# Seven products for eight: up and gate of a feed-forward layer by Strassen's blocks, with a row swap through DRAM

## What is computed

```python
x = fwht(x * SU_ug) / SCALE                        # 2048 rows x 512, "rotated"
x_up = x @ W_up.T * (Wscale_ug[:INTER] * SCALE)    # INTER = 2048
x_gate = x @ W_gate.T * (Wscale_ug[INTER:] * SCALE)
x = jax.nn.silu(x_gate) * x_up
x = fwht(x * SU_dp) / SCALE
x = x @ W_down.T * (Wscale_dp * SCALE)             # back to width 512, added to the rows
```

## Time and profile before

| | us |
|---|---|
| median of 3 runs (1525.26 to 1638.5) | 1525.43 |
| the profiled execution | 1520.79 |
| its span, first to last instruction | 1519.0 |
| granted TensorE clock, mean | 0.992 of full |

### The profile page before, as it was taken

How to read it: one execution, slowest core, us unless ns; L and a number is a source line. 1 busy time by engine, 2 the same in 40 slices (tenths; PEclk the granted TensorE clock), 3 DMA queues, 4 the chain that set the end, 5 groups by cost and what they waited for, 6 DMA issues and landing times. The chain is left out here.

```text
span 1519.0 us, 25272 instructions
## 1 busy us (share of the span) xinstructions
PE 1459.3 (96%) x10520; PEld 988.2 (65%) x10520; DVE 997.7 (66%) x1552; ACT 748.3 (49%) x926; POOL 46.1 (3%) x66
## 2 busy tenths in 40 slices
PE   6999999899999999999899999999999999999998
PEld 5886333677333687333687333677888888888886
DVE  5853999786999784999784999573333324334333
ACT  4344899335999435899335999322221212112111
POOL 1000000110000100000100000100000000000000
PEclk9999999999999999999999999999999999999999
DMA  8453000555000443000543300631010101000002
GB/s 267 151 186 125 9 10 9 153 170 194 9 9 10 153 142 139 9 10 9 154 150 148 157 10 9 200 120 56 28 55 2 56 0 55 28 28 28 1 28 83
DMA packets 53051, 120.01 MB, mean 79 GB/s; under 512 B 11472, under 2 KB 33248, under 8 KB 48080
## 3 DMA queue, kind: packets, MB, share of 16 engines
q1 hardware_dynamic: 41632, 69.94, 13.4%
q0 software_dynamic: 11312, 48.55, 10.1%
HBM read 81.56 MB, written 36.90 MB: 78 GB/s over the span
## 5 line engine op out<-in xcount | busy, mean ns | idle before, releaser
L958 ACT ACTIVATE cx_probs<-cx_sc,proj_mbias 128x1024 f32<-128x1024 f32 (+1 forms) x416 | 442.3, 1113 | 43.8 <-PE cx_sc L1221 34.8
L1103 DVE TENSOR_SCALAR cx_probs<-cx_probs 128x1024 f32<-128x1024 f32 (+1 forms) x416 | 269.9, 685 | 55.4 <-ACT cx_probs L958 54.0
L1065 DVE TENSOR_TENSOR cx_padd<-cx_probs,cx_probs 128x1024 f32<-128x1024 f32 x192 | 233.9, 1218 | 1.2 <-DVE cx_probs L1103 0.4
L1221 PEld LDWEIGHTS cx_sc<-cx_q,cx_kt 32*128 32x128 f32 (+1 forms) x2496 | 102.9, 182 | 197.1 <-ACT cx_probs L958 180.3
L1234 PE MATMUL cx_acc<-cx_probs,cx_vt 128*32 128x512 f32 (+1 forms) x1664 | 220.4, 602 | 3.8 <-DVE cx_probs L1103 3.8
L1221 PE MATMUL cx_sc<-cx_q,cx_kt 32*128 32x512 f32 (+1 forms) x2496 | 204.8, 430 | 14.7 <-ACT cx_probs L958 11.3
L136 PE MATMUL cx_sc<-proj_cs,proj_wk 128*128 128x256 f32 (+1 forms) x1152 | 148.7, 289 | 11.2 <-DVE proj_wk L614 11.2
L136 PEld LDWEIGHTS cx_sc<-proj_cs,proj_wk 128*128 128x128 f32 x1152 | 146.2, 192 | 14.2 <-issue 12.9
L136 PE MATMUL cx_sc<-proj_wv,proj_cs 128*128 128x512 f32 (+1 forms) x624 | 150.4, 397 | 5.2 <-DVE cx_kt L1048 5.2
L136 PEld LDWEIGHTS cx_sc<-proj_wv,proj_cs 128*128 128x128 f32 (+1 forms) x624 | 113.5, 184 | 35.3 <-DVE cx_kt L1048 5.4
L1246 PE MATMUL cx_tot<-cx_padd,cx_ones 128*32 128x256 f32 x1536 | 120.9, 390 | 0.0
(11 more groups left out here) (238 smaller groups left out, 1678.3 us busy)
## 6 DMA issues: line engine op xcount, KB each, us to landing
proj_raw<-in_ctxT SPq DMA_DIRECT2D x20, 512.0 KB, 4.8
scr_q<-cx_q SPq DMA_DIRECT2D x3, 2048.0 KB, 7.1
cx_wo<-scr_wo POOLq DMA_DIRECT2D x3, 2048.0 KB, 14.0
scr_xs<-cx_xs POOLq DMA_DIRECT2D x3, 2048.0 KB, 7.9
cx_q<-scr_q SPq DMA_DIRECT2D x3, 1536.0 KB, 9.1
cx_qxt<-in_x SPq DMA_DIRECT2D x4, 1024.0 KB, 8.9
scr_wd<-cx_wdhi POOLq DMA_DIRECT2D x4, 1024.0 KB, 6.6
scr_wd<-cx_wdlo POOLq DMA_DIRECT2D x4, 1024.0 KB, 8.2
```

The lines of the kernel that those rows point to most:

```text
L958: nc.scalar.activation(prob(N)[0:r], sc[n % NSC][0:r], ACT.Exp, bias=mbias[0:r, b, t:t + 1], scale=SCALE).then_inc(exp_done, 1)
L1065: nc.vector.tensor_tensor(padd[z][(g * QP + j) % 2][:], prob(2 * i + z)[:], prob(2 * i + 2 + z)[:], ALU.add).then_inc(added[z], 1)
L1103: nc.vector.tensor_scalar(prob(N)[0:r], prob(N)[0:r], LOW, HIGH, ALU.max, ALU.min).then_inc(clip_done, 1)
L1221: last = nc.tensor.matmul(sc[(2 * i + h // 2) % NSC][0:r, h % 2], kt[own, z, c, t * P:t * P + r], q[own, y, c], start=n == 0, stop=n == 2)
```

## The change

All groups but the first (groups 1 to 7) compute up and gate in another way. The stage is now a pair of batches in a group: n = 0 to 13, group 1 + n // 2, batches 0 and 1 for even n, 2 and 3 for odd. The output of a pair for up (w = 0) or gate (w = 1) is a matrix of 2 x 2 tiles (2 blocks of columns by 2 batches), with an inner dimension of 2 halves. Strassen's scheme (in the form with 4 sums of the left blocks and 4 of the right ones) makes it from 7 products of blocks, each with 2 chunks, so 6 matmuls, where there were 4 tiles of 12.

The left factors are the weights: class `Sums` loads four raw blocks (128 x 256 each, by POOL), makes four sums of them on DVE (S1 to S4), and ACT and DVE split all seven at once (128 x 1792). The right factors are the rotated rows: class `Turned` makes its sums once for each pair (eight DVE operations of 128 x 1024) and splits four of them. For the pair 0 and 1 this lies in the first group (`beside`), for the pair 2 and 3 mostly in stage 0.

The products run in the order 1, 5, 6, 2, 7, 3, 4 into three banks: 1, 6, 7, 4 add up in one, 5 and 3 in another, 2 in a third. ACT copies a bank after products 1, 5 and 6 into `kept` (`copies`), and DVE adds to `kept` the banks after 2, 7 and 3 (`sum_of`). Product 6 waits for the copy of 1, 7 for that of 6, 3 for that of 5, 4 for the sum over 7. Gate's banks are up0, gp0, up1; up's are gp1, yp2, yp3. The first product of a gate waits only for the silus of the stage before (`silu_done`), the first of an up for its weightings (`hf_done`), and up's product 5 for the accumulation of all row tiles (`y_read`). `copies` of a gate also waits until the weightings of the stage before have read `kept`.

PE's order is gate products of n, the row tiles of n - 1, up products of n. A row tile is now 6 matmuls (both blocks at once) and counts for itself; there are eight in a stage. Stage 13's row tiles stand behind the last products. The rows `x1` have two buffers instead of four, and SP stores and loads them (1 MB each way) around each half stage, through DRAM. The down weights of a group are single-buffered and come over POOL. The groups stand in the program one after the other, without the loop.

```diff
+class Sums:
+    ORDER = (1, 5, 6, 2, 7, 3, 4)
+    LEFT = {1: A11, 2: A12, 3: S4, 4: A22, 5: S1, 6: S2, 7: S3}
+    BANK = {1: 0, 6: 0, 7: 0, 4: 0, 5: 1, 3: 1, 2: 2}
...
+    def load(self, eng, io, g, w):
+        src = io[("upT", "gateT")[w]].rearrange("(c p) n -> p c n", p=P)
+        for block, inner, half in ((self.A11, 0, 0), (self.S3, 1, 0), (self.A22, 1, 1), (self.A12, 0, 1)):
+            n = (g * GC + inner) * P
+            eng.dma_start(self.raw(w, block), src[:, 2 * half:2 * half + 2, n:n + P]).then_inc(self.raw_in[w], 16)
+    def add(self, nc, dve, g, w):
+        v = nc.vector
+        base = ((g - 1) * 2 + 1 - w) * self.STEPS
+        dve.wait_ge(self.raw_in[w], g * 4 * 16)
+        v.tensor_tensor(self.raw(w, self.S1), self.raw(w, self.S3), self.raw(w, self.A22), ALU.add).then_inc(self.step, 1)
+        dve.wait_ge(self.step, base + 1)
+        v.tensor_tensor(self.raw(w, self.S3), self.raw(w, self.A11), self.raw(w, self.S3), ALU.subtract).then_inc(self.step, 1)
+        v.tensor_tensor(self.raw(w, self.S2), self.raw(w, self.S1), self.raw(w, self.A11), ALU.subtract).then_inc(self.step, 1)
+        dve.wait_ge(self.step, base + 3)
+        v.tensor_tensor(self.raw(w, self.S4), self.raw(w, self.A12), self.raw(w, self.S2), ALU.subtract).then_inc(self.step, 1)
...
+class Turned:
...
+    def right(self, product, t):
+        n = {5: 1, 6: 2, 7: 3, 4: 4}
+        if product in n:
+            return self.place(n[product], t)
+        return {1: self.x1[:, t, 0:2], 2: self.x1[:, t, 2:4], 3: self.x2[:, t, 2:4]}[product]
+    def add(self, nc, dve, k):
+        x1, x2 = (x.bitcast(F32) for x in (self.x1, self.x2))
+        x11, t1, t2, t3, t4 = self.spare[:, 0], self.whole(1), self.whole(2), self.whole(3), self.whole(4)
+        out, a, b, alu, needs = (
+            (x11, x1[:, 0, 0:2], x1[:, 1, 0:2], ALU.add, 0),
+            (t3, x2[:, 0, 0:2], x2[:, 1, 0:2], ALU.add, 0),
+            (t2, x2[:, 0, 2:4], x2[:, 1, 2:4], ALU.add, 0),
+            (t1, t3, x11, ALU.subtract, 2),
+            (t3, t2, t3, ALU.subtract, 4),
+            (t2, t2, t1, ALU.subtract, 5),
+            (t4, x1[:, 0, 2:4], t2, ALU.subtract, 6),
+            (t4, t4, x1[:, 1, 2:4], ALU.add, 7))[k]
+        at_least(dve, self.step, needs)
+        nc.vector.tensor_tensor(out, a, b, alu).then_inc(self.step, 1)
...
+        part_banks = [[gp[1], yp[2], yp[3]], [up[0], gp[0], up[1]]]
+        row_banks = [yp[2], yp[3], yp[0], yp[1]]
...
+                for s, b in enumerate(BATCHES):
+                    later = [x for x in BATCHES[s + 1:] if x % 2 == b % 2]
+                    if s < len(BATCHES) - B:
+                        sp.wait_ge(y_read, (s + 1) * ST)
+                        sp.dma_start(scr["x1"][b], x1[b % 2][:]).then_inc(rows_out, 16)
...
+                        sp.wait_ge(rows_out, (s + 1) * 16)
...
+                    if later:
+                        load_rows(later[0])
...
+                pool.wait_ge(chain.c_done, B * HC)
+                sums.load(pool, io, 1, 1)
+                sums.load(pool, io, 1, 0)
+                pool.wait_ge(down_done, UN)
+                load_down(1)
+                for g in range(2, GR):
+                    n = (g - 1) * PAIRS - 1
+                    pool.wait_ge(part_done, parts(n, 1, 4))
+                    sums.load(pool, io, g, 1)
+                    pool.wait_ge(part_done, parts(n, 0, 4))
+                    sums.load(pool, io, g, 0)
+                    pool.wait_ge(down_done, downs(n))
+                    load_down(g)
...
+                def copies(n, w):
+                    act.wait_ge(hf_done, units(n - 1))
+                    if w == 0:
+                        act.wait_ge(silu_done, units(n))
+                    for k, product in enumerate((1, 5, 6)):
+                        act.wait_ge(part_done, parts(n, w, product))
+                        nc.scalar.activation(kept[k][:], part_banks[w][Sums.BANK[product]][:], ACT.Copy).then_inc(copied, 1)
+                def gate(n):
+                    copies(n, 1)
+                    for k, (src, need, value) in enumerate((
+                            (kept[0], summed, three(n, 1, 1)), (kept[1], summed, three(n, 1, 2)),
+                            (kept[2], summed, three(n, 1, 3)), (part_banks[1][0], part_done, parts(n, 1, 4)))):
+                        col = group_of(n) * GC + KEYS[k][0]
+                        act.wait_ge(need, value)
+                        nc.scalar.activation(gates[k][:], src[:], ACT.Silu, scale=scale[:, 1, col:col + 1]).then_inc(silu_done, 1)
+                def upper(n):
+                    copies(n, 0)
+                    if n == 0:
+                        turned[1].split_hi(nc, act, 4)
+                    for k in range(HELD):
+                        act.wait_ge(hf_done, units(n, k + 1))
+                        nc.scalar.activation(held[k][:, 0], weighed[k][:, 1], ACT.Copy).then_inc(h_hi, 1)
...
+                for n in range(SU):
+                    gate(n)
+                    if n == 0:
+                        for k in (1, 2, 3):
+                            turned[1].split_hi(nc, act, k)
+                    elif n % PAIRS == 0:
+                        sums.split_hi(nc, act, group_of(n), 0)
+                    elif n < SU - 1:
+                        sums.split_hi(nc, act, group_of(n) + 1, 1)
+                    upper(n)
...
+                def sum_of(n, w, k):
+                    product = (2, 7, 3)[k]
+                    dve.wait_ge(part_done, parts(n, w, product))
+                    dve.wait_ge(copied, three(n, w, k + 1))
+                    nc.vector.tensor_tensor(kept[k][:], part_banks[w][Sums.BANK[product]][:], kept[k][:], ALU.add).then_inc(summed, 1)
+                def weigh(n, k):
+                    src, need, value = ((kept[k], summed, three(n, 0, k + 1)) if k < 3 else (part_banks[0][0], part_done, parts(n, 0, 4)))
+                    col = group_of(n) * GC + KEYS[k][0]
+                    dve.wait_ge(need, value)
+                    dve.wait_ge(silu_done, units(n, k + 1))
+                    if k == 0:
+                        dve.wait_ge(down_done, downs(n - 1))
+                    nc.vector.scalar_tensor_tensor(weighed[k][:, 1], src[:], scale[:, 0, col:col + 1], gates[k][:],
+                                                   ALU.mult, ALU.mult).then_inc(hf_done, 1)
+                def split_lo(n, k):
+                    dve.wait_ge(h_hi, units(n, k + 1))
+                    nc.vector.tensor_tensor(held[k][:, 1], weighed[k][:, 1], held[k][:, 0].bitcast(F32), ALU.subtract).then_inc(h_lo, 1)
+                def gate(n):
+                    for k in range(3):
+                        sum_of(n, 1, k)
+                def upper(n):
+                    sum_of(n, 0, 0)
+                    weigh(n, 0)
+                    sum_of(n, 0, 1)
+                    weigh(n, 1)
+                    if n == 0:
+                        for k in (2, 3):
+                            turned[1].split_lo(nc, dve, k)
+                    split_lo(n, 0)
+                    sum_of(n, 0, 2)
+                    weigh(n, 2)
+                    split_lo(n, 1)
+                    weigh(n, 3)
+                    split_lo(n, 2)
+                    split_lo(n, 3)
+                def downs_of(n):
+                    g = group_of(n + 1)
+                    if n + 1 < SU and (n + 1) % PAIRS == 0:
+                        sums.add(nc, dve, g, 0)
+                    accumulate(B + 2 * n)
+                    if n + 1 < SU and (n + 1) % PAIRS == 0:
+                        sums.split_lo(nc, dve, g, 0)
+                    if n + 2 < SU and (n + 1) % PAIRS:
+                        sums.add(nc, dve, g + 1, 1)
+                    accumulate(B + 2 * n + 1)
+                    if n + 2 < SU and (n + 1) % PAIRS:
+                        sums.split_lo(nc, dve, g + 1, 1)
...
+                for k in range(1, 5):
+                    turned[1].add(nc, dve, k)
+                gate(0)
+                accumulate(LAST)
+                for k in range(5, 8):
+                    turned[1].add(nc, dve, k)
+                turned[1].split_lo(nc, dve, 1)
+                upper(0)
+                turned[1].split_lo(nc, dve, 4)
+                for n in range(1, SU):
+                    gate(n)
+                    downs_of(n - 1)
+                    upper(n)
+                downs_of(SU - 1)
...
+                def products(n, w):
+                    tu = turned[n % PAIRS]
+                    pe.wait_ge(sums.lo_done[w], group_of(n))
+                    for product in Sums.ORDER:
+                        bank = part_banks[w][Sums.BANK[product]]
+                        if product == 1:
+                            if w == 0:
+                                pe.wait_ge(hf_done, units(n - 1))
+                            elif n:
+                                pe.wait_ge(silu_done, units(n - 1))
+                            else:
```

(35 more changed lines are left out.)

363 lines of the change are left out of this document (198 added, 165 removed).

## The result

| | before | after |
|---|---|---|
| median, us | 1526.71 | 1508.95 |
| the profiled execution | 1520.79 | 1508.34 |
| its span | 1519.0 | 1506.5 |
| first matmul of `ffn` to the end of the span | 559.6 | 544.7 |
| granted TensorE clock, mean | 0.992 | 0.990 |

The ratio of after to before is 0.9886 (95% interval 0.9857 to 0.9915): 17 us or 1.1% faster. The interval does not contain 1, and the gain is under 2%. The median before counts one execution of 1638.5 us in a slower state of the chip, which the ratio leaves out. The fourth line is worked out from starts in the two traces. It leaves the part ahead of `ffn` out, in which only one small load grew (all column scales, 128 bytes a partition where it was 16) and which ended 2.4 us later in the profiled execution of after (961.82 against 959.42; over all kernels of this study it ended between 957.4 and 963.1).

What follows compares the result with a forecast made beforehand. TensorE, without idle time in the feed-forward part, bounds the kernel. 1520.8 - 38.15 + 10.1 + 8.25 + 2.6 - 1.8 = 1501.8; with 4.6 for the median 1506.4, say 1506.5 us, range 1494 to 1521.

Steps and rivals of the forecast that it cites:

- What goes: Up and gate in seven of eight groups: 168 matmuls go, each worth its TensorE slot of 0.2271 us: -38.15 us.
- Slots: Products and row tiles: slot depends on how often the bank changes, 0.2271 to 0.233; together nothing, bounds -2.6 to +6.9.
- The stall: Twelve steady stages: gate's product 6 waits 0.71 us for ACT's late copy, 0.84 with the slower block behind: +10.1 us.
- Rival A: Steady stages: no stalls, by more overlap or 0.7 us of slack; 10.1 and half of the start go: 1492; chance 0.12.
- Rival B: Stages: evacuating banks costs more, with longer waits in gate and up halves, +15: 1521 us; chance 0.16.
- The start: First group and first stages: delays of 0.22 and 1.14, then waits of 1.4, 2.2 and 2.9 (instead of 0.71): +8.25 us.
- The end: Last row tiles wait for the third low part, +2.6 us; behind the last matmul four accumulations shrink to one, -1.8.
- Rival C: Raw gate blocks land late, so up's product 5 waits; slower than before from 11.5 us after issue; chance 0.04.

## Why the prediction was right, point by point

The change is faster by less than 2%, as forecast, the median lies in the range 1494 to 1521, and the predicted 1506.5 is 2.5 below it. That it is so close is luck, since two errors partly cancel: the sum for the profiled execution (1501.8) was 6.5 too low, and the 4.6 that I added for the median was not there (the median of after is 0.6 above its profiled execution).

| term, us | predicted | measured |
|---|---|---|
| 168 matmuls at 0.2271 | -38.15 | -38.15 |
| slots of products, row tiles, first group | 0 | +5.0 |
| stalls of the steady stages | +10.1 | +8.8 |
| the start | +8.25 | +9.2 |
| wait ahead of the last row tiles | +2.6 | +2.7 |
| behind the last matmul | -1.8 | -2.1 |
| sum, and `ffn` from the traces | -19.0 | -14.6, -14.85 |
| ahead of `ffn` | 0 | +2.4 |

- **What goes.** Right: the matmuls were taken from a PE that had no wait, and twelve stages with product 3 twice gave the slots back. The 131 ns of the Trainium skill (TensorE: Matmul & The Clock Gate, Back-to-back issue gap) would have made 22 us of them; the trace had 227 before and has 227 to 234 after.
- **Slots.** This step failed. "The slot depends a little on how often the bank changes" was a line through two rows that differed in two things at once. With `hs` moved by 480 bytes three matmuls to a bank are as fast as twelve. By the line, products would be dearer and row tiles cheaper; both were dearer: 0.2300 instead of 0.2271 on the mean of the products (+3.4), 0.2343 instead of 0.2329 for down (+1.0), and 0.233 for 96 matmuls of the first group (+0.6). My bounds of -2.6 to +6.9 held it, by luck of the arithmetic and not by the mechanism.
- **The stall.** Right in place, in cause and in number of stages. I put the last weighting at 1.45 behind the end of the up products, its high part at 2.24, the copy at 2.77 to 3.37, product 6 at 3.43. The trace has 1.39, 2.16, 2.70 to 3.28 and 3.33. Product 6 was due at 2.76, not 2.72, since its predecessors are dearer; on the mean of the twelve, 0.62 of gap and 0.11 of restart are 0.73 where I had 0.84. Rival A (no stalls) needed 0.7 us of slack in that line, and there was 0.1. Rival B (waits in both halves) did not come: no wait stands in any up half after the first.
- **The start.** The three waits were forecast at 1.4, 2.2 and 2.9; the profile has 1.17, 2.01 and 2.81. What was missing is the clock: 1.6 us behind the third. The first group's two waits went from 1.10 and 1.94 to 0.94 and 2.92, where I had forecast 0.22 and 1.14 more:

```profile
1014.53 3.06 PE L136 MATMUL ff_up<-ff_xs,hand_ugs 128*128 128x512 f32 x12 [0.94 <-DVE ff_hf L1719]
...
1024.18 0.66 PE L399 MATMUL ff_up<-all_ident,ff_xn 128*128 128x128 f32 x4 [2.92 <-ACT ff_xT L274]
```

- **The end.** Right. PE waits 2.82 for the last low part, and of the accumulations only one stands behind the last matmul: it ends 1.1 us behind that one's start (1503.46 + 0.69, against 1503.03), where four ended 2.9 behind it before; the other 0.3 of the 2.1 lies behind the accumulation:

```profile
1491.94 11.48 PE L136 MATMUL ff_yp<-hand_wds,ff_held 128*128 128x512 f32 x48 [2.82 <-DVE ff_held L1754]
```

```profile
1503.46 0.69 DVE L1677 TENSOR_TENSOR ff_x<-ff_yp,ff_x 128x512 f32<-128x512 f32 x1 [0.72 <-PE ff_yp L136]
```

- **Rival C.** Right not to weigh much, but for a wrong price: a block of 128 KB landed in 2.6 us, not in the 4.6 of half a megabyte that I had taken for four together. The Trainium skill (DMA: Bandwidth & Descriptors, Anatomy of one DMA) gives 2.0 us and the bytes at 436 GB/s, for 128 KB an estimate of 2.3; the trace of after agrees within 0.3. The later issue, beside a 1 MB store, showed 4.6 for the same DMA.

## What to carry to other kernels

When a change takes work from a full engine, write out the orders of the engines that feed it over one period, with start-to-start spacings from rows: here that gave the wait of a steady stage to 0.1 us and those of the start to 0.2, and it shows the repair too (a copy moved ahead of one operation was worth 8 us, where the whole change had brought 17). A wait of 2 us must be priced with what the clock may do behind it; one that recurs in each stage can double in price. When like instructions differ by 3% in two places, look for everything in which the places differ before drawing a line through them: a change that adds a tile moves all the tiles behind it.

## What the runs showed of the hardware

- A matmul of 128 x 512 takes 0.2267 us when its stationary and its moving tile start at the same remainder of 256 bytes, and 0.232 to 0.2343 when they do not (difference of 32: 0.2329; of 416: 0.2337 to 0.2343; of 384, which is a multiple of 128: 0.232 to 0.233). Right behind a slower block or a wait the first few take more in either case. It was 5.0 us of the kernel before and 8.2 of the changed one, by the traces.
- TensorE fell from its level of 2.4 GHz to that of 1.2 GHz at waits of 2.0 to 3.0 us in `ffn` in some places and executions and not in others, and at the seven of 3.8 to 4.4 each time: of the same three waits of the start, behind the third in the changed kernel, behind the second and third with 416 bytes of padding, behind the second with two low parts moved. Where a wait of 2.1 to 2.2 recurred every 34 us, it happened in nine of twelve stages. In most cases seven or eight matmuls took 0.427 instead of 0.227, in two cases twelve or thirteen. At waits of 0.9 to 1.6, and at those of 0.4 to 0.6 in twelve stages of seven kernels, it did not happen once.
- A DMA of 128 KB took 2.5 to 2.8 us by itself or beside the end of a 1 MB load of the rows, and 4.2 to 4.9 when it was issued within 2 us behind a 1 MB store of the rows.
